# Decayed attention: the causal mask made by GpSimd on the exponentials, and the first tile's copies made by VectorE

## What is computed

```python
def _L3_attn_ref(x, w_qkv, w_o, log_xi):          # 8 batches of 256 tokens, 16 heads of 8
    ...
    q = pi * _rotate(q, cos, sin) + (1.0 - pi) * q
    k = pi * _rotate(k, cos, sin) + (1.0 - pi) * k
    d_mat = jnp.abs(pos[:, None] - pos[None, :])
    decay = -e * d_mat[None, :, :] / xi[:, None, None]
    causal = jnp.where(pos[:, None] >= pos[None, :], 0.0, -jnp.inf)
    bias = decay + causal[None, :, :]
    scores = jnp.einsum('bhqd,bhkd->bhqk', q, k) * dh ** (-0.5) + bias[None]
    attn = jax.nn.softmax(scores, axis=-1)
    out = jnp.einsum('bhqk,bhkd->bhqd', attn, v)
    return out.reshape(b, n, H * dh) @ w_o
...
x = _layernorm(x + _L3_attn_ref(x, L3_attn_w_qkv, L3_attn_w_o, L3_attn_log_xi), axis=-1)
x = _layernorm(x + _L3_ffn_ref(x, L3_ffn_weight, L3_ffn_alpha, L3_ffn_bias), axis=-1)
```

## Time and profile before

| | us |
|---|---|
| median of 3 runs | 1761.07 |
| lowest, highest of them | 1760.69, 1762.39 |
| time of the profiled execution | 1756.33 |
| its span, from first to last instruction | 1754.5 |
| TensorE, VectorE, ScalarE, GpSimd busy in the span | 1509.9, 1004.8, 860.9, 636.9 |

### The profile page before, as it was taken

One profiled execution on the slowest core, in us unless ns is written; L12 is line 12 of the kernel. 1 busy time (PEld: TensorE's weight loads), 2 busy tenths in 40 slices (PEclk: granted clock), 3 DMA queues, 4 the chain that ended last, 5 costly groups with the idle time before them and its releaser, 6 DMA issues. The chain is left out here.

```text
span 1754.5 us, 31069 instructions
## 1 busy us (share of the span) xinstructions
PE 1509.9 (86%) x11186; PEld 1104.7 (63%) x11187; DVE 1004.8 (57%) x2367; ACT 860.9 (49%) x1888; POOL 636.9 (36%) x712
## 2 busy tenths in 40 slices
PE   4689978799987899996839999899987999778996
PEld 3356656466664566775827787788876576545664
DVE  6656536665466789996035554366655222435555
ACT  5455544556456867773424444544443233235552
POOL 3387702877240767772230000100013602411113
PEclk8789989899989889998969999999997999879998
DMA  8300000000001565544334000000000111300000
GB/s 228 111 7 19 13 7 2 13 13 13 13 1 27 87 80 77 77 61 111 84 89 134 1 0 1 1 1 1 1 1 1 46 45 32 36 4 2 2 2 25
DMA packets 75920, 64.45 MB, mean 37 GB/s; under 512 B 25627, under 2 KB 63050, under 8 KB 75790
## 3 DMA queue, kind: packets, MB, share of 16 engines
q1 hardware_dynamic: 65790, 54.32, 14.9%
q0 software_dynamic: 3072, 6.30, 1.8%
q10 hardware_dynamic: 6928, 2.12, 0.6%
HBM read 48.88 MB, written 9.58 MB: 33 GB/s over the span
## 5 line engine op out<-in xcount | busy, mean ns | idle before, releaser
L1315 POOL TENSOR_TENSOR inject<-delta_x,b_rows 128x512 f32<-128x512 f32 x128 | 160.2, 1277 | 65.2 <-DVE delta_x L1612 37.6
L1639 DVE TENSOR_TENSOR_SCAN state<-bank,inject 128x512 f32<-128x512 f32 x128 | 149.9, 1206 | 7.5 <-issue 5.2
L2072 POOL TENSOR_TENSOR ve<-mv,eps 128x1 f32<-128x1 f32 x32 | 6.1, 190 | 335.9 <-DVE mv L2220 335.9
L1544 ACT ACTIVATE bank<-delta,a_neg 128x255 f32<-128x255 f32 x256 | 108.9, 472 | 6.8 <-DVE state L1639 6.1
L3334 DVE TENSOR_REDUCE top<-bank 128x2 f32<-128x512 f32 (+1 forms) x96 | 61.8, 686 | 72.4 <-PE bank L3036 51.6
L2181 ACT ACTIVATE Z<-bank 128x512 f32<-128x512 f32 x64 | 34.7, 595 | 128.7 <-PE bank L2134 128.7
L2158 ACT ACTIVATE U<-bank 128x512 f32<-128x512 f32 x128 | 74.6, 593 | 40.8 <-PE bank L2095 39.7
L611 POOL TENSOR_TENSOR rotated<-rot_cos,rot_sin 128x512 f32<-128x512 f32 x56 | 70.8, 1269 | 52.6 <-DVE rot_sin L917 52.6
L1419 PEld LDWEIGHTS bank<-tabs,by_token 128*128 128x128 f32 x512 | 68.7, 198 | 25.2 <-issue 15.1
L617 POOL TENSOR_TENSOR inv_norm<-sum_sq,neghalf 128x16 f32<-128x16 f32 x28 | 82.0, 2929 | 4.2 <-POOL sum_sq L615 0.3
L654 PE MATMUL bank<-wqkv,hT 128*128 128x512 f32 x128 | 68.7, 667 | 14.0 <-ACT hT L815 11.3
(11 more groups left out here) (565 smaller groups left out, 4142.8 us busy)
## 6 DMA issues: line engine op xcount, KB each, us to landing
b_rows<-rows_dram SPq DMA_DIRECT2D x32, 512.0 KB, 8.7
v<-v SPq DMA_DIRECT2D x32, 130.0 KB, 2.3
slots<-zero SPq DMA_DIRECT2D x10, 256.0 KB, 3.6
rows<-slots SPq DMA_DIRECT2D x10, 256.0 KB, 4.1
moe_w<-in_L_ffn_rg_dram SPq DMA_DIRECT2D x1, 2048.0 KB, 8.4
moe_w<-in_L_ffn_ru_dram SPq DMA_DIRECT2D x1, 2048.0 KB, 13.6
wqkv<-in_L_ffn_wqkv_dram SPq DMA_DIRECT2D x2, 768.0 KB
slots_out<-y SPq DMA_DIRECT2D x8, 160.0 KB, 2.1
```

The lines of the kernel that those rows point to most:

```text
L1315: pool.tensor_tensor(dB[:, n % R, :, :], dx[:, :, seq(n)], both(b_all[:, q % 4, n % CH, :]), ALU.mult).then_inc(s.inject.sem, 1)
L1544: last = act.activation(dA[n % RD][:, c, 1:L], delta[:, c, i * L + 1:(i + 1) * L], ACT.Exp, scale=a_neg[:, c, k:k + 1])
L1639: dve.tensor_tensor_scan(flat(h[:, n % R, :, :]), flat(dA[n % RD]), flat(dB[:, n % R, :, :]), 0.0, ALU.mult, ALU.add).then_inc(s.state.sem, 1)
```

## The change

Masks of the exponentials. `mask(i, c)` is gone. The last product of `shifted` now reports `shifted`, so the exponentials are made of all scores, also those above the diagonal. GpSimd has a new step `causal(i, c)`: it waits for the four exponentials of chunk c and goes over both squares of `prob` in place by `affine_select`, 4 heads by 128 columns each, which keeps a value where query minus key is not negative and writes 0 elsewhere. `mix` waits for it (`causal`), where it had waited for the exponentials.

Copies of the first tile. k and q of the first tile are copied from the banks by VectorE (`copy_first`), before its reductions; those of the second tile stay with ScalarE. The signal `qkT` is split into `qk_first` and `qk_second`, and the waits follow.

Order on GpSimd. The casts come in two halves with the selects among them, and in the last turn the selects stand among the norms of the ternary layer. The order of all other steps is kept.

```diff
     FEW = 3
-    s = open_stage(nc, net, "clear:2 rate0:1 rate:1 decay:1 proj:2 v_ready:2 products:2 wide:2 turned:4 qkT:4 "
-                   "cast:4 scored:12 maxed:12 top16:1 top_parts:1 top_ps:1 top_row:1 shifted:16 exped:16 mixed:2 o_wide:2 o_ps:2 "
+    s = open_stage(nc, net, "clear:2 rate0:1 rate:1 decay:1 proj:2 v_ready:2 products:2 wide:2 turned:4 qk_first:2 qk_second:2 "
+                   "cast:4 scored:12 maxed:12 top16:1 top_parts:1 top_ps:1 top_row:1 shifted:16 exped:16 causal:4 mixed:2 o_wide:2 o_ps:2 "
                    "row_inv:2 o_ready:2 oT_ps:1 oT_ready:1 " + NORM +
...
     turn_bank = lambda m: X[1 - m % 2]
+    copied = lambda i, m: (s.qk_first if m < 2 else s.qk_second).at(i, m % 2 + 1)
+    copies = lambda m: (s.qk_first if m < 2 else s.qk_second).sem
...
         def _(pool):
-            def cast(i, p):
+            def causal(i, c):
+                pool.wait_ge(s.exped.sem, s.exped.at(i, HPG * (c + 1)))
+                for at in (0, L):
+                    of = prob[:, c, :, at:at + P]
+                    last = pool.affine_select(of, of, [[0, HPG], [1, P]], ALU.is_ge, pool.to_reg(0.0), base=0, channel_multiplier=-1)
+                last.then_inc(s.causal.sem, 1)
+
+            def cast(i, p, first=0):
                 pool.wait_ge(s.scored.sem, s.scored.at(i, 0))
-                for m, (which, t) in enumerate(TURN):
+                for m, (which, t) in enumerate(TURN[first:first + 2], first):
                     to, of = (k16, kT[p]) if which == "k" else (q16, qT[p])
-                    pool.wait_ge(s.qkT.sem, s.qkT.at(i, m + 1))
+                    pool.wait_ge(copies(m), copied(i, m))
                     settle(pool, s)
             def run(i, p, ahead, behind):
-                if ahead:
-                    cast(i + 1, 1 - p)
+                causal(i, 0)
+                cast(i + 1, 1 - p)
+                causal(i, 1)
+                cast(i + 1, 1 - p, 2)
+                causal(i, 2)
+                causal(i, 3)
                 if behind:
...
             cast(0, 0)
+            cast(0, 0, 2)
             for i in range(B - 1):
                 run(i, i % 2, min(2, B - 1 - i), i > 0)
-            for k in range(B - 2):
-                tern_rstd(k)
+            causal(B - 1, 0)
+            causal(B - 1, 1)
+            tern_rstd(0)
+            tern_rstd(1)
+            causal(B - 1, 2)
+            tern_rstd(2)
+            tern_rstd(3)
+            causal(B - 1, 3)
+            tern_rstd(4)
+            tern_rstd(5)
             norm_rstd(pool, s, n, B - 2)
...
-                    pe.wait_ge(s.qkT.sem, s.qkT.at(i, m - 1))
+                    pe.wait_ge(copies(m - 2), copied(i, m - 2))
...
                 for y in range(HPG):
-                    pe.matmul(S[y][:, L:SPAN], kT[p][row(y), c, P:L], qT[p][row(y), c, P:L], start=False, stop=False)
-
-            def mask(i, c):
-                for y in range(HPG):
-                    masked = S[y].rearrange("p (h q) -> p h q", h=2)[:, :, 0:P]
-                    pe.matmul(masked, net.ident16[:, :], diagonal.unsqueeze(1).to_broadcast([P, 2, P]), start=False, stop=True)\
+                    pe.matmul(S[y][:, L:SPAN], kT[p][row(y), c, P:L], qT[p][row(y), c, P:L], start=False, stop=True)\
                         .then_inc(s.shifted.sem, 1)
             def mix(i, p, half):
-                pe.wait_ge(s.exped.sem, s.exped.at(i, 2 * HPG * (half + 1)))
+                pe.wait_ge(s.causal.sem, s.causal.at(i, 2 * (half + 1)))
                 for c in (2 * half, 2 * half + 1):
...
                 shifted(i, p, 0)
-                mask(i, 0)
                 if not ahead:
...
-                mask(i, 1)
...
                     ternary(2)
-                mask(i, 2)
                 if not ahead:
...
-                    pe.wait_ge(s.qkT.sem, s.qkT.at(i + 1, 3))
+                    pe.wait_ge(copies(2), copied(i + 1, 2))
...
                     score_top(i + 1, 6, 7)
-                mask(i, 3)
                 if ahead:
                     mask_top(i + 1, 6, 7)
-                    pe.wait_ge(s.qkT.sem, s.qkT.at(i + 1, 4))
+                    pe.wait_ge(copies(3), copied(i + 1, 3))
                 else:
...
                 mask_top(0, u, u + 1)
-            pe.wait_ge(s.qkT.sem, s.qkT.at(0, 4))
+            pe.wait_ge(copies(3), copied(0, 3))
             for t in ORDER:
...
-                act.activation(to[:, :, tok(t)], turn_bank(m).rearrange("p (c t) -> p c t", t=P), ACT.Copy).then_inc(s.qkT.sem, 1)
+                act.activation(to[:, :, tok(t)], turn_bank(m).rearrange("p (c t) -> p c t", t=P), ACT.Copy).then_inc(s.qk_second.sem, 1)
...
                 if ahead:
-                    for m in range(4):
+                    for m in (2, 3):
                         copy_qk(i + 1, 1 - p, m)
...
                 take(0, 0, t)
-            for m in range(4):
+            for m in (2, 3):
                 copy_qk(0, 0, m)
...
+            def copy_first(i, p):
+                for m in range(2):
+                    which, t = TURN[m]
+                    dve.wait_ge(s.turned.sem, s.turned.at(i, m + 1))
+                    to = kT[p] if which == "k" else qT[p]
+                    dve.tensor_copy(to[:, :, tok(t)], turn_bank(m).rearrange("p (c t) -> p c t", t=P)).then_inc(s.qk_first.sem, 1)
+
             def highest(i, u):
...
                 if ahead:
+                    copy_first(i + 1, 1 - p)
                     for u in range(8):
...
             rotate(0)
+            copy_first(0, 0)
             for u in range(12):
```

## The result

The changed kernel took 1748.03 us (median of four runs, 1747.87 to 1749.52), the kernel before on the same chip 1761.73 (1760.69 to 1765.06). The ratio is 0.9921, 95% interval 0.9904 to 0.9938: 13.7 us faster, between 11 and 17. Predicted were 1749.2, with 1744 to 1765 as the range, and 0.77 for faster. Of all executions told of here one, of the kernel with the select twice, took 3646.65 us; nothing kept says why, and that kernel's median and ratio leave it out.

The account below looks back on a forecast made before the run. TensorE was taken to bound the turn, with the select adding 0.3 us at the second mix. Seven turns' 13.3 less 1.2 and 0.2 gives 11.9: 1756.33 becomes 1744.4, plus 4.7 to the median 1749.2 us; range 1744 to 1765.

Parts of the forecast that it names:

- masks of chunks 0 and 1 ahead of the first tile's scores: Before the first reduction: removing two groups of mask matmuls, 0.45 us each, takes 0.90 us off directly.
- the wait for the cast: TensorE's wait before the first tile's scores for GpSimd's cast of q: falls from 0.83 to 0.1 us.
- TensorE itself comes to the second mix: Without the select, TensorE would reach the second mix 16.3 us after the turning of the maxima.
- I take 0.9, closest to 0.77: GpSimd's select, shown in no row: priced 0.9 us from multiply-and-add's 0.77, with ends 0.61 and 3.3.
- the prediction's own formula: Steady turn as 18.75 + 2a us, a being one select's price; at 0.9 it gives 20.55.
- the floor of 20.2: Steady turn can't fall under 20.2 us, held there by TensorE and the reductions' two banks.
- the rival of the cheap select: Select at 0.75 us or less: TensorE and the reductions' banks hold the turn, total 1745 to 1746.6; chance 0.17.
- VectorE's copies: First tile's k and q copied by idle VectorE before its reductions, priced 0.69 us each like its reductions.
- 6 us for each us of a: Last turn: selects queue before GpSimd's scalings, starting them 1.2 us later; 6 us per us of select price a.
- The clock of 0.83 in that stretch is left as it is: Last turn: TensorE's granted clock of 0.83 was assumed unchanged.
- seven steady turns: Last stage: seven turns, each 1.90 us shorter, counted as 13.3 us gained.
- The clock rival: A longer wait at the second mix lowers TensorE's clock in each turn, total 1761; chance 0.05.

Follow-up runs that it names:

- masks-only kernel: Changed kernel with ScalarE making all copies again, GpSimd still masking: 1757.34 us, ratio to before 0.9938, steady turn 21.31.
- fillers' kernel: Changed kernel plus unread matmuls, 16 in the first turn and twice 20 around the last turn's second mix: 1747.33 us, ratio to before 0.9931.
- both norms first: Changed kernel with batch 6's and the last batch's norm powers moved ahead of ternary-layer ones on GpSimd, last turn: 1746.82 us, ratio to before 0.9919.
- the repeat: The changed kernel run once more, unedited: 1754.15 us, ratio to before 0.9929, steady turn 20.57.
- three groups: Follow-up kernels ran in three groups, each on one chip beside the kernel before, whose medians were 1766.52, 1759.07 and 1760.32 us.
- half reductions: Changed kernel with VectorE's reductions over half of the keys, output not the reference's: 1737.65 us, ratio to before 0.9880, steady turn 19.84.

## Why the prediction was right, and where it wasn't

Point by point, each in us, and from the turn's L3047 or L3069 where it is a place:

| step | predicted | measured |
|---|---|---|
| masks of chunks 0 and 1 ahead of the first tile's scores | 0.90 off | 0.61 off |
| the wait for the cast | 0.83 to 0.10 | 0.83 to 0.09 |
| first reduction | 8.05 | 8.33 |
| exponentials of chunk 3 begin | 13.1 | 13.51 |
| a select | 0.9 | 0.637 |
| TensorE itself comes to the second mix | 16.3 | 16.61 |
| second mix | 16.6, after waiting 0.3 | 16.61, no wait |
| second mix to the next turning | 3.95 | 3.97 |
| turn | 20.55 | 20.58 |
| GpSimd's scalings in the last turn | 1.2 later | 0.6 earlier, with another clock |
| opening | +0.2 | +0.13 |

**The select was mis-sized.** The step is "I take 0.9, closest to 0.77". By the prediction's own formula, 18.75 + 2 x 0.637 = 20.0, so under the floor of 20.2: the rival of the cheap select, 1745 to 1746.6. It measured like a cast with one input, not like the multiply and add. The 0.77 row was the wrong neighbour; the select takes 0.024 us more than the cast. The Trainium skill ("GPSIMD Engine Reference", "Performance pitfalls for Q7 kernels") has 1.03 or 2.03 cycles an element for a compare-and-select, the estimate of 0.44 or 0.87 us plus the fixed part. The measured 0.637 lies under the higher even without a fixed part, so only the lower agrees, and it would leave 0.20 for the fixed part, which no run here measured apart. The branching body of its section "Elementwise — side-by-side cycle accounting", an estimate of 5.1 us, is excluded for this operation by the same row.

**The floor was mis-sized as well, the other way.** TensorE comes to the second mix at 16.61, not at 16.3. Nearly all of that is in one step: "Those of chunks 0 and 1 stand before the first reduction, so 0.90 comes off that part directly". It was 0.61. In the kernel before, TensorE's products of chunks 1 and 2 in the turn of rows 2:

```profile
1656.00 0.50 PE L3055 MATMUL bank<-minus_top,pick 32*128 32x384 bf16 x4
...
1658.98 0.90 PE L3055 MATMUL bank<-minus_top,pick 32*128 32x384 bf16 x4
```

The products of chunk 1 write to the same four banks S from which ScalarE is reading the exponentials of chunk 0. These begin 1652.62 - 1650.47 = 2.15 after the turning, where they began at 2.37: only 0.22 earlier, since they had started behind the first of the four mask matmuls and hadn't waited for all four. TensorE comes to chunk 1 at 1653.94 - 1650.47 = 3.47 against 3.90, 0.43 earlier, and then needs 0.71 for the same first four matmuls, where the kernel before shows 0.50. It comes to chunk 2 at 6.27 against 6.88. So with the masks gone TensorE runs into ScalarE. The program has a wait in front of each of these four matmuls, for the exponential that last read its bank, and the rows of TensorE's weight loads name it. Of the load for the fourth matmul:

```profile
1654.32 0.09 PEld L3077 LDWEIGHTS bank<-minus_top,pick 32*128 32x128 bf16 x1 [0.28 <-ACT prob L3260]
```

That load begins 1654.32 - 1650.47 = 3.85 after the turning, just as the products behind the four matmuls do; in the kernel before those begin at 4.07. That is 0.22 earlier, as much as the exponentials. The masks-only kernel shows the same wait of 0.28 and the same 0.62 without the copies, so the loss isn't from VectorE or the casts. No kernel here had other banks. From the first reduction to the second mix the prediction had 8.25 by TensorE alone, measured were 8.28: the 0.15 for chunk 2's mask and the 0.45 for chunk 3's hold as a sum. Chunk 3's exponentials are 0.41 later than forecast: 0.28 by this place and 0.12 because they begin 1663.98 - 1662.96 = 1.02 after the shifted products, for which 0.9 was taken.

**The errors met at one number, and that is luck.** With the select at 0.9, and all else as measured, the mix would have been late by about 0.5 (two selects 0.53 longer, 0.02 of room). With the floor as forecast, the turn would have been 20.2. It came out at 20.57, 0.02 from the forecast, because a wait of 0.3 that didn't come stood on a floor 0.3 too low. The select's own chain came out right by the same luck: its pair takes 1.23 and not 1.74, but chunk 3's exponentials are 0.4 later and the hand-over to the mix is 0.14 where 0.05 was taken, so by it too the mix can't begin before 16.6. The forecast time of a turn was right, its named bound was not: the kernel without selects has the same turn, and the one with shorter reductions has 0.73 less.

**VectorE's copies** came out as worked: 0.692 each. From chunk 2's products to the first tile's scores it took 1.54 in the kernel before, the wait of 0.83 taken off (1660.52 - 1658.98), and 1658.37 - 1656.74 = 1.63 now. So 0.09 is left of the wait, though the row names none; q's cast ends at 1658.32, 0.05 before the scores. One term was off: from the end of the first copy (1656.15 + 0.69 = 1656.84) to GpSimd's cast at 1657.00 it is 0.16, where 0.05 was taken from the hand-over to TensorE. From q's copy to its cast it is the same, and one such step stands in the chain that TensorE waits for. Those 0.11 us more than cover the 0.09 that is left of the wait.

**The last turn.** "6 us for each us of a" gives 6 x (0.637 - 0.9) = -1.6 to the 1.2, so 0.4 earlier; measured was 17.68 against 18.32 after the turning, 0.6 earlier. But these two executions aren't alike. The kernel before had the clock's fall at the start of that turn (0.66 from 1720 to 1725), the changed kernel had 1.00 from 1712 to 1727. So chunk 1's exponentials ended 6.77 after the turning and not 8.52, 1.8 earlier where 0.9 was counted; and GpSimd, which the sum had busy without a gap, stood idle 0.66 before chunk 3's selects. The fillers' kernel has GpSimd's order of the changed one and the early fall: its scalings start at 18.58, 0.3 later than before. Of that the formula's 0.4 earlier and the gap of 0.66 are the sum. So the queue on GpSimd was read rightly; the select's price was too high in it, and the gap was missing. The last turn didn't become shorter. It is 35.61 against 35.04, and the time went behind the scalings. They start in the changed kernel at 1729.87, here with chunk 3's selects, and TensorE's two waits:

```profile
1725.84 1.22 POOL L2955 TENSOR_SCALAR_AFFINE_SELECT prob<-prob 128x512 f32<-128x512 f32 x2 [0.66 <-ACT prob L3260]
...
1729.87 4.97 POOL L2992 TENSOR_SCALAR x_tok<-x_tok,t_mv,t_rstd 128x128 f32<-128x128 f32 x6
```

```profile
1727.21 0.64 PE L3089 MATMUL bank<-prob,v 128*32 128x256 f32 x8 [1.57 <-POOL prob L2955]
...
1730.70 0.44 PE L220 MATMUL bank<-tabs,n_xn 128*128 128x128 f32 x2 [1.98 <-DVE n_xn L194]
```

The stretches behind it, in the changed kernel and then in the kernel before:

```profile
1725.00:1730.00 5.00, 2.15 (x38) 1.48 (x36) 1.66 (x10) 1.37 (x4) 4.10 (x10) 1.00 0.01 2
1730.00:1735.00 5.00, 3.27 (x17) 2.46 (x18) 4.25 (x17) 0.77 (x2) 4.88 (x7) 0.77 0.14 43
1735.00:1740.00 5.00, 2.18 (x10) 1.71 (x9) 1.99 (x8) 0.00 (x0) 1.75 (x4) 0.50 0.40 115
```

```profile
1740.00:1745.00 5.00, 2.75 (x21) 2.12 (x19) 2.81 (x14) 0.38 (x1) 4.05 (x8) 1.00 0.43 125
1745.00:1750.00 5.00, 1.88 (x6) 1.21 (x6) 2.32 (x9) 0.38 (x1) 0.46 (x1) 0.55 0.11 32
```

In the kernel before, the scalings start at 1737.78, and TensorE's two waits ahead of them were:

```profile
1735.59 0.64 PE L3072 MATMUL bank<-prob,v 128*32 128x256 f32 x8 [0.15 <-ACT prob L3247]
1738.61 0.44 PE L220 MATMUL bank<-tabs,n_xn 128*128 128x128 f32 x2 [1.52 <-DVE n_xn L194]
```

TensorE now waits 1.57 for chunk 3's selects and 1.98 for batch 6's norm, which stands behind two pairs of the ternary layer's on GpSimd. After that its clock falls to 0.77 and 0.50 (1.2 GHz), where before it was at 1.00 until 1745, and the products run slower: from the scalings to the end it is 17.9 us against 16.7. The prediction had "The clock of 0.83 in that stretch is left as it is", which failed (in the last 31.0 us it is 0.76 now). The kernel without selects has a last turn of 33.49, and the one with both norms first 33.19. How much of those 2.4 us is the clock and how much the wait isn't separated. The kernel before, the one without selects and the one with both norms first had the early fall and kept 1.00 longer behind the second mix; the changed kernel in three executions had neither. So the 0.57 us by which the last turn grew isn't put down to the selects alone by these runs.

**The first turn** was counted as one of "seven steady turns", and isn't steady. It gave 0.23 in the profiled execution, where the clock was at 0.72 in its first 5 us and fell to 0.75 again later, and 22.93 - 20.24 = 2.7 in the repeat. That makes most of the difference between the two stages, 10.8 and 12.7 less than before; the forecast 11.9 lies between them. The medians differ by 13.7, 12.4 and 10.7 in the three groups, which their intervals don't tell apart.

**The clock rival** had a chance of 0.05 in the turns and didn't come there. "TensorE's share stays" was a fair reason while no wait grew. With a wait of 1.20 it came in three of six steady turns, with one of 0.96 (half reductions) in none.

## What to carry to other kernels

When an edit takes work off an engine that hands its banks to another, ask when the other engine really started before: if it had begun behind the first of four instructions, removing all four brings it forward by one, and the engine that was relieved runs into it. For an operation that no trace shows, keep two neighbours in the sum and not one; and let the formula say from which price on it decides (by the runs, 0.65 us for a select, 0.01 above what it takes), since that tells how much the choice is worth. When the total comes out right, ask each term: here the turn was right to 0.02 us and its bound was another. In a tail where one engine does many small steps for two chains, the order of the steps can be worth as much as the steps: moving two pairs of 0.96 us made the last turn 2.4 us shorter in the traces, part of it perhaps the clock's, and too little to tell over whole runs. And before two executions' tails are compared, see that the clock fell in the same places in both.

## What the runs showed that I had not expected

- A select by index in place on 128x512 in fp32 costs GpSimd 637 ns (636 to 647 over 64 of them), 4% more than its cast of the same shape.
- GpSimd's cast begins 0.16 us after the end of VectorE's copy. TensorE's scores begin 0.05 after the end of the cast, in the same turn, but the mix that waits for a select 0.14 after its end.
- After a wait of TensorE of 1.20 us in a turn of 22 its clock fell in three of six steady turns, to 0.66 to 0.75 in stretches of 5 us. The same wait in the other three cost only itself.
- The same program's first turn took 22.70, 22.71 and 20.24 us in three executions. In the first the clock was at 0.72 in the turn's first 5 us and at 0.75 in a later stretch, in the third at 0.99 and 1.00.
